# Seven experts' down-products in one pass over both parts of W2, with lists as contiguous floats

## What is computed

```
xn  = layernorm(x2)                                  # 2048 tokens x 256
tok = top_idx.T                                      # 8 experts x 512 slots: token numbers
h   = gelu(xn[tok] @ W1[e] + b1[e])                  # 512 x 1024 per expert
out_e = h @ W2[e] + b2[e]                            # 512 x 256 per expert
w   = combine_weights[tok, e]
out = x2 + sum over slots of out_e * w, added to the token's row
```

## Time and profile before

| | |
|---|---|
| time, median of 3 runs | 277.7 us (277.69 to 277.87) |
| the profiled execution | 277.88 us |
| its span | 276.1 us |
| TensorE busy | 266.3 us, 96%, 1698 matmuls |
| TensorE weight loads | 237.0 us, 86% |
| VectorE busy | 222.7 us, 81% |
| ScalarE busy | 180.1 us, 65% |
| GpSimd busy | 161.7 us, 59% |
| chain that ended last | TensorE 81%, VectorE 8%, GpSimd 3% |

### The profile page before, as it was taken

The page is one execution under the profiler, slowest core; times in us unless marked ns, Lnnn a source line. Parts: engine busy times, 40 slices in busy tenths (PEclk is TensorE's granted clock), DMA queues, the critical chain, the costliest instruction groups (busy, mean ns, idle before and its releaser), DMA issues.

```text
span 276.1 us, 5494 instructions
## 1 busy us (share of the span) xinstructions
PE 266.3 (96%) x1698; PEld 237.0 (86%) x1698; DVE 222.7 (81%) x526; ACT 180.1 (65%) x341; POOL 161.7 (59%) x153
## 2 busy tenths in 40 slices
PE   6899999999989999999999999999999999999992
PEld 2689899999866989989899899899899899999992
DVE  1988999899986599978878797797887979777552
ACT  2688899886767765766666658567575675763540
POOL 4475766656835945647556457655645746604555
PEclk9999999999999999999999999999999999999999
DMA  6993258496564755635554544654446451100021
GB/s 199 358 275 100 87 143 226 129 260 225 160 197 131 286 153 157 198 117 170 154 200 147 142 141 140 188 174 138 153 133 199 155 156 69 57 21 33 34 78 69
DMA packets 30293, 42.45 MB, mean 154 GB/s; under 512 B 5251, under 2 KB 24015, under 8 KB 30148
## 3 DMA queue, kind: packets, MB, share of 16 engines
q1 hardware_dynamic: 25392, 30.00, 34.7%
q0 software_dynamic: 4608, 12.24, 14.9%
q10 hardware_dynamic: 276, 0.00, 0.1%
HBM read 33.54 MB, written 9.24 MB: 155 GB/s over the span
## 4 chain that ended last, share of the span: by engine, by line
PE 81%; DVE 8%; issue 4%; POOL 3%; ACT 2%; DMA 1%; DVEq 0%; POOLq 0%; ACTq 0%
PE bank L1155 22%; PE bank L1157 22%; PE bank L1156 22%; PE bank L1199 3%; PE bank L1244 3%; PE bank L1296 2%; PE bank L1315 1%; PE bank L1319 1%; PE bank L1316 1%; DMA x_all<-in_x_dram 1%; POOL out_dram L546 1%; DVE bn L754 1%; PE bank L1151 1%; PE bank L1228 1%; PE bank L1164 1%
## 5 line engine op out<-in xcount | busy, mean ns | idle before, releaser
L731 ACT ACTIVATE keysT<-bank,biasT 128x512 f32<-128x512 f32 x63 | 43.5, 690 | 65.4 <-PE bank L1157 55.0
L546 POOL DMA_INDIRECT out_dram<-h,sidx x32 | 38.5, 1205 | 37.5 <-DVE h L1045 30.5
L537 POOL DMA_INDIRECT x_all<-out_dram,idx_all x32 | 39.4, 1232 | 24.3 <-DMA out_dram<-h,sidx 16.8
L1155 PE MATMUL bank<-x_hi,w_hi 128*128 128x512 f32 (+1 forms) x114 | 45.2, 397 | 0.0
L1157 PE MATMUL bank<-x_hi,w_lo 128*128 128x512 f32 (+1 forms) x114 | 44.2, 388 | 0.0
L1156 PE MATMUL bank<-x_lo,w_hi 128*128 128x512 f32 (+1 forms) x114 | 44.1, 387 | 0.0
L533 POOL DMA_INDIRECT x_all<-token_rows,idx_all x28 | 29.8, 1066 | 19.2 <-DVE factor L1096 8.7
L1052 DVE SCALAR_TENSOR_TENSOR junk<-idx_rows,idx_f,normed 128x512 bf16<-128x512 bf16 (+1 forms) x32 | 38.6, 1206 | 3.0 <-POOL normed L557 3.0
L1078 DVE TENSOR_TENSOR w_lo<-w_raw,w_hi 128x512 fp32r<-128x512 f32 x56 | 38.4, 685 | 0.0
L1157 PE MATMUL bank<-w_hi,g_lo 128*128 128x256 f32 x128 | 36.2, 283 | 0.0
L1156 PE MATMUL bank<-w_lo,g_hi 128*128 128x256 f32 x128 | 36.2, 283 | 0.0
(11 more groups left out here) (172 smaller groups left out, 713.1 us busy)
## 6 DMA issues: line engine op xcount, KB each, us to landing
w_raw<-in_L_ffn_W_dram SPq DMA_DIRECT2D x32, 512.0 KB
idx_rows<-in_L_ffn_top_idx_dram SPq DMA_DIRECT2D x8, 256.0 KB, 4.1
out_dram<-x SPq DMA_DIRECT2D x8, 256.0 KB, 3.0
hn_cnat<-in_ctx_dram SPq DMA_DIRECT2D x7, 256.0 KB, 2.8
token_rows<-xn SPq DMA_DIRECT2D x7, 256.0 KB, 2.2
hn_cnat<-in_L_ffn_b_dram SPq DMA_DIRECT2D x1, 1024.0 KB, 6.6
x_all<-in_x_dram SPq DMA_DIRECT2D x3, 256.0 KB, 4.6
x_all<-in_x_dram SPq DMA_DIRECT2D x1, 768.0 KB, 8.3
```

The lines of the kernel that those rows point to most:

```text
L537: g.indirect_dma_start(accg[:, t, :], None, flat, list_of(e, t)).then_inc(acc_in[t], 16)
L546: g.indirect_dma_start(flat, idx(sidx[:, t:t + 1].bitcast(U32), 0), newrow[:, t, :], None, bounds_check=N - 1, oob_is_err=False).then_inc( ...
L731: a.activation(g32[:, f % NG, :], ps_up[f % 2][:, :], ACT.Gelu_apprx_tanh, bias=bias)
L1155: t_.matmul(dst, lhs_hi, rhs_hi, start=first, stop=False)
```

## The change

Both parts of the weights now lie in one tensor, so that one moving operand can name the high and the low part of the same W2 columns. In experts 0 to 6 a tile's down step is two passes: high part of the gelu times both parts (512 columns, into the whole bank, high products in columns 0 to 255, cross products in 256 to 511), then the low part of the gelu times the high part (256 columns, added into columns 0 to 255). Expert 7 keeps three passes. VectorE adds the cross half of each bank to the sums before it adds the first half: eight instructions instead of four in `new_sums` for experts 0 to 6, in the order c0, c1, n0, c2, n1, c3, n2, n3. Down step 7 of the previous expert moves ahead of up step 1.

The lists: ScalarE copies an expert's list to a contiguous row of floats (`list_f`, which reuses `x_plus_h`), at f = 3 of the expert before; for expert 0 at its own f = 0. The slot totals read that.

```diff
-        w_hi = sb("w_hi", [P, 2, WC], F32R)
-        w_lo = sb("w_lo", [P, 2, WC], F32R)
+        w_parts = sb("w_parts", [P, 2, 2, WC], F32R)
+        w_hi = w_parts[:, :, 0, :]
+        w_lo = w_parts[:, :, 1, :]
...
+        ps_down_cross = [b[:, H:2 * H] for b in banks[4:8]]
+        ps_down_both = [b[:, :].rearrange("p (n h) -> p n h", n=2) for b in banks[4:8]]
+        list_f = x_plus_h
...
+            def list_as_floats(e, s):
+                a.copy(list_f[:, s, :], rows_by_expert[:, ds(e, 1), :].rearrange("p a c -> p (a c)"))\
+                    .then_inc(list_rdy, 1)
...
                         a.copy(w_hi[:, 1 - s, col], w_raw[:, col]).then_inc(whi_rdy, 1)
+                        if is_first(e) and f == 0:
+                            act.wait_ge(x2_rdy, NPAIR)
+                            act.wait_ge(idxrows_in, 16 * IDX_PARTS)
+                            list_as_floats(0, 0)
+                        if f == 3:
+                            if not is_first(e):
+                                act.wait_ge(tot_rdy, NT * e)
+                            list_as_floats(e + 1, 1 - s)
...
-            def new_sums(e, tiles):
-
+            def cross_terms(e, t):
+
+                dve.wait_ge(accb_rdy, NT * e + t + 1)
+                dve.wait_ge(out_mm, NT * e + t + 1)
+                v.scalar_tensor_tensor(accg[:, t, :], ps_down_cross[t], factor[:, t:t + 1], accg[:, t, :],
+                                       ALU.mult, ALU.add).then_inc(cross_rdy, 1)
+
+            def new_sums(e, tiles, crossed=True):
+
+                if crossed:
+                    cross_terms(e, 0)
                 for t in tiles:
+                    if crossed and t + 1 < NT:
+                        cross_terms(e, t + 1)
+                    if crossed:
+                        dve.wait_ge(cross_rdy, NT * e + t + 1)
                     dve.wait_ge(accb_rdy, NT * e + t + 1)
                     dve.wait_ge(out_mm, NT * e + t + 1)
                     v.scalar_tensor_tensor(newrow[:, t, :], ps_down[t], factor[:, t:t + 1],
                                            accg[:, t, :], ALU.mult, ALU.add).then_inc(new_rdy, 1)
...
-                v.scalar_tensor_tensor(junk[:, :], rows_by_expert[:, ds(e, 1), :].rearrange("p a c -> p (a c)"),
-                                       idx_f[:, ds(t * NE + e, 1)], seen[:, t, :], ALU.is_equal, ALU.mult,
+                v.scalar_tensor_tensor(junk[:, :], list_f[:, s, :], idx_f[:, ds(t * NE + e, 1)], seen[:, t, :], ALU.is_equal, ALU.mult,
                                        accum_out=total[:, t:t + 1]).then_inc(tot_rdy, 1)
...
                         if is_first(e) and n == 0:
-                            dve.wait_ge(idxrows_in, 16 * IDX_PARTS)
...
+                        if n == 0:
+                            dve.wait_ge(list_rdy, e + 1)
+                        slot_total(e, s, n)
...
-                    last = three_passes(ps_down[t], g_hi[f % NG][:, g], g_lo[f % NG][:, g], w_hi[:, s, c],
-                                        w_lo[:, s, c], f == 0, f == NF - 1)
+                    if is_last(e):
+                        last = three_passes(ps_down[t], g_hi[f % NG][:, g], g_lo[f % NG][:, g], w_hi[:, s, c],
+                                            w_lo[:, s, c], f == 0, f == NF - 1)
+                    else:
+                        t_.matmul(ps_down_both[t], g_hi[f % NG][:, g], w_parts[:, s, :, c], start=(f == 0), stop=False)
+                        last = t_.matmul(ps_down[t], g_lo[f % NG][:, g], w_hi[:, s, c], start=False,
+                                         stop=(f == NF - 1))
...
                 if not is_first(e):
                     down(e - 1, 1 - s, NF - 2)
+                    down(e - 1, 1 - s, NF - 1)
                 up(e, s, 1)
-                if not is_first(e):
-                    down(e - 1, 1 - s, NF - 1)
```

More of the change, by code:

```diff
@@ L263, in build_xattn_moe @@
         accb_rdy = sem("bias_added_to_sums")
+        cross_rdy = sem("cross_terms_added_to_sums")
         new_rdy = sem("new_sums_ready")
+        list_rdy = sem("list_as_floats_ready")
         tot_rdy = sem("slot_totals")
@@ L714, in _ @@
             x_hi_part(0, 0)
+            rows_by_expert = idx_rows[:, :].rearrange("p (c e) -> p e c", e=NE)
+            def list_as_floats(e, s):
+                a.copy(list_f[:, s, :], rows_by_expert[:, ds(e, 1), :].rearrange("p a c -> p (a c)"))\
+                    .then_inc(list_rdy, 1)
             def expert(e, s, use):
@@ L1046, in new_sums, with slot_total @@
                                            accg[:, t, :], ALU.mult, ALU.add).then_inc(new_rdy, 1)
-            rows_by_expert = idx_rows[:, :].rearrange("p (c e) -> p e c", e=NE)
-            def slot_total(e, t):
-                v.scalar_tensor_tensor(junk[:, :], rows_by_expert[:, ds(e, 1), :].rearrange("p a c -> p (a c)"),
-                                       idx_f[:, ds(t * NE + e, 1)], seen[:, t, :], ALU.is_equal, ALU.mult,
+            def slot_total(e, s, t):
+                v.scalar_tensor_tensor(junk[:, :], list_f[:, s, :], idx_f[:, ds(t * NE + e, 1)], seen[:, t, :], ALU.is_equal, ALU.mult,
                                        accum_out=total[:, t:t + 1]).then_inc(tot_rdy, 1)
@@ L1092, in expert @@
                             dve.wait_ge(tot_rdy, n)
-                        slot_total(e, n)
+                        if n == 0:
+                            dve.wait_ge(list_rdy, e + 1)
+                        slot_total(e, s, n)
                     if part == NF - 3:
@@ L1116, in _ @@
             for t in range(NT):
-                new_sums(LAST, range(t, t + 1))
+                new_sums(LAST, range(t, t + 1), crossed=False)
                 if t + 1 < NT:
```

## The result

The changed kernel takes 276.15 us (median of 7 executions) against 277.72 us before: 1.6 us less, ratio 0.9931 with a 95% interval of 0.991 to 0.9952. The forecast was 276.3, range 275.2 to 277.9. Two later comparisons gave 276.24 against 277.84 and 276.32 against 277.95. So here its stretches are compared, not its span.

The account below looks back on a forecast made before the run. TensorE was taken to pace every expert (23.34 us, no idle time). With 1.4 us off its down steps and all else hidden, span 276.1 became 274.7; plus 1.78 around it, less 0.18, gave 276.3 us, range 275.2 to 277.9.

Parts of the forecast that it names:

- TensorE's tile: Down steps of seven experts: merging two passes saves 6 ns a tile, 1.4 us in 224 tiles; bounds 0.5 and 1.8.
- The issue-gap rule: Interval between TensorE's passes: columns over 2.4 GHz plus about 2.5 ns, making the merge worth only 0.56 us.
- Rival 1: Down steps: the merged pass costs two passes, 0.236 us; time 277.7, or 277.2 at the upper value; 16%.
- The cover of the sums: Change of expert: VectorE's eight operations end at +6.04 us, TensorE needs the fourth tile at +6.58; hidden, 0.5 to spare.
- Rival 2: Next expert's first down step: TensorE waits for sums at 0.61 us an operation; 283.2 us; 11% with anything like it.
- The moved down step: Down step 7 ahead of up step 1: outputs 1.4 us earlier, no work added, nothing for TensorE in itself.
- Slot totals: VectorE, four per expert: 1201 ns falls to 804, 1.6 us saved per expert, off the path except a 0.3 us stall.
- The list copy: ScalarE, one more copy per expert: some 0.6 us, perhaps twice that from the stride; hidden, costs nothing.

Follow-up runs that it names:

- x1: Changed kernel with three 256-column passes again and no cross terms, keeping float lists and moved down step: 278.01 us.
- x2: Changed kernel with the 512-column pass written as two 256-column passes, cross half and eight VectorE operations kept: 279.78 us.
- x0: The changed kernel itself, run again beside x1 to x3 on the same chip: 276.24 us, ratio to before 0.992 to 0.996.
- x7: Changed kernel with weight parts in turns of 256 high and 256 low columns, so the 512-column operand is contiguous: 276.41 us.
- x3: Changed kernel with down step 7 back behind up step 1: 277.66 us.
- x5: Changed kernel with each new sum right behind the cross term it needs (c0, n0, c1, n1, ...): 277.50 us.
- x6: Changed kernel with strided lists and down step 7 behind up step 1, so the merge and cross terms alone: 278.61 us.
- x4: Changed kernel with slot totals reading the strided integer lists as before, without ScalarE's copy: 276.85 us.
- x8: Changed kernel with 11 instead of 9 warm-up matmuls on zeros, plus 2 before the first transposes: 276.31 us.
- x9: The longer warm-up kernel of x8 run once more: 276.28 us.

## Why the prediction was right

- **TensorE's tile**: right in mechanism, and the size a little small. I took 6 ns a tile from three down blocks of 1.43, 1.41 and 1.41 us; x1 and x2 against x0 give 8, the upper bound I had named (1.8 us in 224 tiles). The three blocks were not typical: the two of 1.41 are the only short ones of a period, the other six take 1.43 to 1.44, as these two of the kernel before, 141.97 to 143.40 and 144.78 to 146.21:

```profile
141.97 0.28 PE L1155 MATMUL bank<-w_hi,M_hi 128*128 128x256 f32 x1
...
143.40 0.39 PE L1155 MATMUL bank<-x_hi,w_hi 128*128 128x512 f32 x1
...
144.78 0.28 PE L1155 MATMUL bank<-w_hi,M_lo 128*128 128x256 f32 x1
...
146.21 0.39 PE L1155 MATMUL bank<-x_hi,w_hi 128*128 128x512 f32 x1
```

All eight down blocks of a period fell from 11.43 to 11.18 us, 8 ns a tile. The whole period fell by 0.23, since the up blocks became 0.01 to 0.02 longer: 1.4 forecast, 1.6 measured. The issue-gap rule of the Trainium skill (TensorE: Matmul & The Clock Gate, section Back-to-back issue gap), cited in the prediction, would give 2.5 ns; x1 and x2 rule that out here. That section gives the rule for an isolated matmul, which the prediction did not say.

- **Rival 1** (a merged pass costs two) fell with x2 and x7.
- **The cover of the sums**: worked out at +6.04 against +6.58, measured +6.03 against +6.57. Rival 2's mechanism, TensorE waiting at the new sums, is real: x3 shows it when the chain starts later. Its price of 0.61 us an operation was too high (0.52, x5).
- **The moved down step**: here the prediction said "nothing for TensorE in itself", which the trace bears out, but it didn't say what the kernel would be without it. x3 and x6 show that the forecast gain depends on it almost wholly (277.66 against 277.84 before, 23.32 against 23.35). So the forecast holds for the change as a whole, which had the cover that the sum worked out, and not for the merge alone. A sum that only asks whether the new work is hidden doesn't show which edit hides it.
- **Slot totals**: 746 ns against the 804 taken; VectorE's busy time as expected. The stall that they remove at expert 1 was put at 0.3 us and measures 0.5: I had missed the low parts of the next rows, which stand in VectorE's queue behind the late totals, and the slower pass behind a stall.
- **The list copy**: 1225 ns, the upper end, and hidden as argued. In expert 0 the first three up blocks take 1.56, 1.52 and 1.50 us, as before the change (1.57, 1.52, 1.50).

## What to carry to other kernels

Where one engine paces a stage without a gap, price a change on it by the distance of instruction starts over every block of a period, not over a few of them, and expect no more than the per-instruction part: here 8 ns for each pass of about 120 that was merged into another. Then look for the consumer that must give a buffer back before the next block, and count the distance in units of the pacing engine's work; moving one block of independent work in between was worth 0.2 us an expert, nearly as much as the merge that it protected. Undo each part alone: the parts of a change that "cost nothing" may be the ones that let the gain through.

## What the runs showed of the hardware

*A stall costs TensorE more than its length.* A 512 pass that had to wait was followed by the next after 0.33 to 0.35 us instead of 0.23, and the 512 pass after that by 0.27 or 0.28 where one came. So a wait of 0.04 us cost 0.20 in x3, one of 0.18 cost 0.34 in x4, and one of about 0.01 cost 0.10 in x5. Why isn't shown.

*From VectorE's sum to TensorE's pass.* A pass that waited for a sum started 0.05 to 0.06 us behind the end of the sum (x3, x4, x5).

*Strided integers.* A read of 512 integers 32 bytes apart costs ScalarE 1225 ns against 623 for a contiguous copy of floats, and VectorE's total 1201 against 746 from contiguous floats. The stride and the number type changed together, and no run separates them. The Trainium skill has a rule for the stride (SBUF — State Buffer, the section Door 1: The DMA port swizzle): reads that go to a new 16-byte line each time pay a penalty. The traces agree with its direction.

*TensorE's clock in the setup.* Three longer executions are traced, and each differs from the shorter ones before 12 us. In the profiled execution of the changed kernel the granted clock was at its lower level (1.2 GHz) from 7.8 to 11.2 us. TensorE had been idle for 0.96 us before the first weights and 0.68 before the first transposes. The stretch from 8 to 10 us of that execution (busy times as above, then the clock), and the second group of weight products:

```profile
8.00:10.00 2.00, 2.00 (x8) 1.57 (x6) 1.29 (x4) 0.59 (x1) 0.00 (x0) 0.50 1.09 348
```

```profile
8.57 1.91 PE L1169 MATMUL bank<-setup_or_probs 128*128 128x256 f32 x4
```

In x0's profiled execution the clock is 1.00 there, after idle times of the same size (1.01 and 0.69 us):

```profile
8.00:10.00 2.00, 2.00 (x10) 1.11 (x8) 1.68 (x7) 1.27 (x3) 0.00 (x0) 1.00 1.09 350
```

```profile
8.24 1.03 PE L1169 MATMUL bank<-setup_or_probs 128*128 128x256 f32 x4
```

The same four matmuls take 1.91 us in the one and 1.03 in the other, and everything behind comes 1.4 to 1.5 us later, up to the first expert. So the length of the idle times alone doesn't decide whether the clock falls.

The other two longer executions (x3's, 279.35 us, and the second one of x2, 279.31) are different. There the first group of weight products is slow already; in x3:

```profile
6.08 2.08 PE L1169 MATMUL bank<-setup_or_probs 128*128 128x256 f32 x4 [0.73 <-DMA setup_or_probs<-in_L_xattn_k_w_dram]
...
8.80 1.92 PE L1169 MATMUL bank<-setup_or_probs 128*128 128x256 f32 x4
```

The first group takes 1.13 us in x0 and in the longer execution above. The durations are those of the lower level, though the clock column has 1.00 there, so in these two the level isn't read from the profile but inferred. It looks as if the clock had not yet risen in them, where in the first it had risen and fell again. The longer warm-up of x8 and x9 may act on either.

The kernel before has longer executions as well (9 of 35 above 278.5 us beside x0 to x3), so long executions are no part of the change; none of that kernel's is traced. The 1.3 to 1.5 us are 0.5% of the time, nearly as much as the effect studied.
